# A two-block attention kernel on one core: the last 64 rows of keys and of queries as one chunk, another order of the jobs, and x's low halves earlier

## The chip, the cores and the metric

The kernel runs on one core of a Trainium2 chip. The metric is the time of one execution on the device, in microseconds, from the profiler; lower is better. The engines are TensorE (PE, its weight loads PEld), VectorE (DVE), ScalarE (ACT), GpSimd (POOL) and SyncE (SP), which here issues all transfers. Each engine runs its own list of instructions in order and waits for others by semaphores.

## The reference

64 independent sequences of 128 tokens, x (64, 128, 320) and a context of 128 tokens by 192. Two blocks, in float32:

```python
# block 0: attention over the context's first 124 tokens (8 heads of 40), a second one
# through its last 4 tokens, then a projection and the residual
query = hidden_states @ Wq
hs = _mha(query, enc @ Wk, enc @ Wv)
ca_q1 = jnp.einsum('btc,th->bch', ca, Wq_ca)[:, indices, :]
ca_hs1 = _mha(ca_q1, residual, residual)
ca_hs2 = _mha(ca_hs1 @ Wq, ca @ Wk_ca, ca @ Wv_ca)
out = (hs + ca_hs2) @ Wout + b_out + residual
# block 1: self attention, cross attention (20 heads of 16), gated feed-forward
h1 = _ln(x, n1_g, n1_b)
x = _attn(h1, h1, q1, k1, v1, o1_w, o1_b, heads) + x
h2 = _ln(x, n2_g, n2_b)
x = _attn(h2, context, q2, k2, v2, o2_w, o2_b, heads) + x
a, g = jnp.split(_ln(x, n3_g, n3_b) @ ff_w1 + ff_b1, 2, axis=-1)
x = a * gelu(g) @ ff_w2 + ff_b2 + x
```

## The kernel before

Two sequences make a step, so there are 32 steps, and the work of three stages is interleaved: while step i is in block 1's attention, the block 0 of the next step and the feed-forward of the step before run beside it. The program is a head (weights are scaled and split into a high and a low half of float16, so that a product in float16 passes comes near float32), step 0, step 1, a loop over 30 passes, step 32, and a tail with the last feed-forward. Steps 0, 1 and 32 are the loop's body with some jobs left out.

A step is a table of jobs, `BODY`, 128 of them. A job fills one of six PSUM banks in turn by matmuls and is evacuated by ScalarE, VectorE or both; a job waits until the job six places earlier in the table has been evacuated (`bank_free`, `last_on_bank`). So the table sets which job waits for which evacuation. The order of each engine's instructions is written out by hand, engine by engine, as calls such as `chunk16`, `scores` or `low_split`.

Names: Q0T k and K0T k are block 0's queries and keys, K1T k and Q1T k self attention's keys and queries, Q2T k and K2T k those of cross attention, each in chunks k = 0, 1, 2; those of block 1 have 128, 128 and 64 rows (`CH1`), a row being one column of a weight matrix. XT j_b are transposed norms (hTn), V0, V1, V2 values, S n and T n the scores for the maxima and for the exponents of unit n (units 0 to 3 the second attention of block 0, 4 to 13 self, 14 to 23 cross, 24 to 27 block 0's first), mx g the transposed maxima, ff t the feed-forward's first product, y b its second, outT and outM an attention's output and its projection, G the gains of the token queries. att is the product of exponents with values.

A chunk of K1T, Q1T or Q2T goes this way: 8 matmuls in `chunk16`; ScalarE writes its high half (`high_shifted`, L890), VectorE the whole value (`whole_shifted`, L1426), GpSimd the low half by a subtraction (`low_split`, L552), and SP spreads the heads over partitions by three transfers (`put_split`, `spread`, L406) into Ks or Qs, from where the scores read. `SPLITS_STEP` counts these chunks, 9 a step. Other GpSimd work named below: `low_probabilities` (L545) makes the low half of the exponents; `deviation` (L602, L603) the reciprocal deviation of a norm; `x_values` (L567 to L569), `token_queries` (L579 to L584, its last instruction writes ca_heads) and `low_x` (L592, the low half x16 of x) prepare the next step's block 0; the argument -1 means step 0, done in the head. `residual` (L1587) and `norm` (L1598) are VectorE's; `gelu` (L961) and `exps` (L977, L978) ScalarE's, which loads another function table between the two kinds.

Of the kernel before, what the change touches and what calls it, by code (L numbers as in the profile page):

```python
# [8 lines left out]
G = 2  # L9
# [83 lines left out]
SPLITS = {"K1T": 0, "Q1T": 3, "Q2T": 6}  # L93
SPLITS_STEP = 9
# [7 lines left out]
V1_FACTOR = 2.0 ** (V_EXP - math.floor(math.log2(1.01 * H * X_SCALE * 2.0 ** (W_EXP + 1))))  # L102

# [89 lines left out]
def build(nc, d, out):  # L193
# [4 lines left out]
    with ctx:  # L198
# [182 lines left out]
        def _(sp):  # L381
# [67 lines left out]
            def one_pass(i, stores, last=False):  # L449
# [4 lines left out]
                put_low(i, "Q0T", 2, Q0s, cQ, Q_PARTS)  # L454
# [2728 lines left out]
```

## Time and profile before

| | us |
|---|---|
| median of 3 runs | 3501.17 (3498.44 to 3502.05) |
| profiled execution | 3492.75 |
| its span, first to last instruction | 3490.9 |
| TensorE busy | 3261.7 (93%) |
| ScalarE busy | 2438.0 (70%) |
| VectorE busy | 2236.2 (64%) |
| GpSimd busy | 2022.1 (58%) |

All rows below come from the profiled execution, so sums are made against its 3492.75 us. Busy times overlap between engines. In a timeline, a row gives the start, the duration and the instruction, and in square brackets the engine's idle time before it with what ended it; rows of equal instructions are merged (x8). Matmuls are pipelined, so a row's duration contains some latency, and the distance between two starts is the time that TensorE spends.

### The profile page before, as it was taken

The numbers are of one execution on the slowest core, as the hardware profiler recorded it, in microseconds if no ns is written. First come the engines' busy times: TensorE is split into PE (matmuls) and PEld (weight loads), VectorE is DVE, ScalarE is ACT, GpSimd is POOL, SyncE is SP. The second block draws the span as 40 slices with busy tenths as digits, with TensorE's granted clock in tenths as the row PEclk, the third lists the DMA queues.
The fourth block names the chain that finished last, engine by engine and source line by source line (L and its number), as shares of the span: only waits on it lengthen the run. The fifth ranks groups of instructions, "written<-read, shape, count | busy, mean of one in ns | idle before, by whom it ended". The sixth has DMA issues, their size and how long they took to land.

```text
span 3490.9 us, 110595 instructions
## 1 busy us (share of the span) xinstructions
PE 3261.7 (93%) x37652; PEld 2674.3 (77%) x37652; DVE 2236.2 (64%) x5366; ACT 2438.0 (70%) x4279; POOL 2022.1 (58%) x2242
## 2 busy tenths in 40 slices
PE   7579999999999999999999999999999999999988
PEld 6367777787877778787777877777777777777766
DVE  6366666667666666766666676666667666666743
ACT  3257777777777777777777777777777777777753
POOL 1355656655665665566566555656655665665552
PEclk7589999999999999999999999999999999999998
DMA  6321111222111122222112222211222211122210
GB/s 196 63 51 44 52 41 45 50 50 57 48 52 42 44 50 51 56 48 54 40 45 50 53 54 48 54 39 45 50 50 57 48 51 41 45 51 50 57 35 19
DMA packets 314756, 181.21 MB, mean 52 GB/s; under 512 B 49740, under 2 KB 313900, under 8 KB 314028
## 3 DMA queue, kind: packets, MB, share of 16 engines
q1 hardware_dynamic: 302457, 172.71, 20.1%
q8 instruction: 323, 5.29, 0.6%
q10 hardware_dynamic: 11955, 3.04, 0.4%
q14 instruction: 21, 0.17, 0.0%
HBM read 69.36 MB, written 24.67 MB: 27 GB/s over the span
## 4 chain that ended last, share of the span: by engine, by line
PE 38%; POOL 26%; issue 26%; DVE 5%; ACT 2%; POOLq 1%; SPq 1%; DMA 1%; DVEq 1%; ACTq 0%
PE bank L2227 35%; POOL PT L545 15%; DVE mx L1525 2%; PE bank L2254 1%; POOL XB L522 1%; POOL XA L522 1%; POOL ca_heads L584 1%; POOL rstd L603 1%; POOL cQ L552 1%; POOL cK L552 1%; POOL c L597 1%; ACT P L977 1%; POOL rstd L602 1%; PE bank L2349 1%; ACT PT L978 1%
## 5 line engine op out<-in xcount | busy, mean ns | idle before, releaser
L545 POOL TENSOR_TENSOR PT<-P,PT 128x512 f16<-128x512 f32 (+1 forms) x896 | 1037.2, 1158 | 435.2 <-ACT PT L978 424.9
L1525 DVE TENSOR_REDUCE mx<-bank 128x4 f32<-128x512 f32 (+1 forms) x896 | 571.4, 680 | 92.0 <-PE bank L2227 88.6
L2227 PE MATMUL bank<-hT,w_ff_w 128*128 128x256 f16 x5120 | 611.1, 274 | 1.4 <-DVEq L1777 1.4
L2227 PEld LDWEIGHTS bank<-hT,w_ff_w 128*128 128x128 f16 x5120 | 498.5, 98 | 68.3 <-issue 6.2
L2227 PE MATMUL bank<-mxs,pick 84*128 84x128 f16 (+1 forms) x3584 | 506.9, 222 | 0.0
L2227 PE MATMUL bank<-w_ff,F 128*128 128x320 f32 x1280 | 393.3, 443 | 1.3 <-DVE F L1604 1.3
L2227 PEld LDWEIGHTS bank<-V,PT 128*128 128x128 f16 (+1 forms) x9216 | 315.3, 96 | 80.4 <-POOL PT L545 48.7
L2227 PEld LDWEIGHTS bank<-mxs,pick 84*128 84x128 f16 (+1 forms) x3584 | 368.3, 105 | 2.9
L2227 PE MATMUL bank<-Qs,Ks 96*128 96x128 f16 x2560 | 357.1, 222 | 9.1 <-DVE mxs L1534 8.8
L2227 PE MATMUL bank<-V,PT 128*128 128x17 f16 (+1 forms) x9216 | 343.3, 173 | 18.7 <-POOL PT L545 17.1
L961 ACT ACTIVATE gate<-bank,ff_b,scale 128x256 f32<-128x256 f32 x320 | 180.6, 564 | 215.0 <-PE bank L2227 175.1
L552 POOL TENSOR_TENSOR cQ<-whole,cQ 128x256 f16<-128x256 f32 (+1 forms) x192 | 128.2, 668 | 296.2 <-DVE whole L1426 287.9
L977 ACT ACTIVATE P<-bank,log_p,held 128x512 f32<-128x512 f32 x320 | 246.0, 769 | 71.8 <-PE bank L2227 40.9
L2227 PEld LDWEIGHTS bank<-w_ff,F 128*128 128x128 f32 x1280 | 227.2, 191 | 69.5 <-DVE F L1604 1.5
L2227 PEld LDWEIGHTS bank<-Qs,Ks 96*128 96x128 f16 x2560 | 247.0, 99 | 23.8 <-DVE mxs L1534 21.4
L977 ACT ACTIVATE P<-bank,log_p,exp_self 128x512 f32<-128x512 f32 x320 | 249.7, 780 | 15.0 <-PE bank L2227 5.5
L1426 DVE TENSOR_SCALAR whole<-bank,q_factor,qk_b 128x256 f32<-128x256 f32 (+1 forms) x288 | 155.8, 541 | 161.7 <-ACT cK L890 92.4
L1604 DVE SCALAR_TENSOR_TENSOR F<-bank,ff_b,gate 128x256 f32<-128x256 f32 x320 | 154.5, 483 | 156.4 <-ACT gate L961 145.8
L978 ACT ACTIVATE PT<-bank,log_p,exp_self 128x512 f16<-128x512 f32 x320 | 250.0, 781 | 0.0
L978 ACT ACTIVATE PT<-bank,log_p,held 128x512 f16<-128x512 f32 x320 | 245.7, 768 | 0.0
L938 ACT ACTIVATE hTn<-bank 128x384 f16<-128x384 f32 x320 | 153.8, 492 | 131.0 <-PE bank L2254 130.7
L2227 PE MATMUL bank<-Ks,Qs 96*128 96x128 f16 x2560 | 214.9, 221 | 17.1 <-DMA Qs<-cQ 12.9
(291 smaller groups left out, 7024.6 us busy)
## 6 DMA issues: line engine op xcount, KB each, us to landing
Qs<-cQ SPq DMA_DIRECT2D x402, 64.0 KB, 2.6
Ks<-scratch_k SPq DMA_DIRECT2D x99, 160.0 KB, 4.9
Ks<-cK SPq DMA_DIRECT2D x198, 64.0 KB, 2.6
Q0s<-cQ SPq DMA_DIRECT2D x198, 60.0 KB
K0s<-cK SPq DMA_DIRECT2D x198, 60.0 KB
xin<-in_x SPq DMA_DIRECT2D x33, 320.0 KB, 3.1
out<-X SPq DMA_DIRECT2D x64, 160.0 KB, 1.9
scratch_k<-cK SPq DMA_DIRECT2D x68, 128.0 KB, 1.9
```

The costliest lines, as they stand in the source:

```text
L522: nc.gpsimd.tensor_tensor(dst[:, b, :], src[:, b, :], bias[:, j, :], ALU.add).then_inc(ready, 1)
L545: nc.gpsimd.tensor_tensor(PT[0:keys, n % PT_SLOTS, 1, :], P[0:keys, n % P_SLOTS, :], PT[0:keys, n % PT_SLOTS, 0, :], ALU.subtract).then_in ...
L552: nc.gpsimd.tensor_tensor(dst[0:r, 1, k, :], whole[0:r, m % 3, :], dst[0:r, 0, k, :], ALU.subtract)\
L584: nc.gpsimd.tensor_tensor(ca_heads[:, :, :], ca16[:, :].unsqueeze(1).to_broadcast([rows, HEADS0, GS]), mask_ca[:, :].unsqueeze(2).to_broad ...
L938: nc.scalar.activation(dst[:, 0:3, b * S:(b + 1) * S], bank[:, 0:3 * S].rearrange("p (k s) -> p k s", k=3), ACT.Copy, scale=scaled).then_i ...
L961: nc.scalar.activation(gate[:, t % 2, :], bank[:, 0:GS], ACT.Gelu, scale=scale[:, 1:2], bias=ff_b[:, FFT + t:FFT + t + 1]).then_inc(a_done, 1)
L977: nc.scalar.activation(P[0:keys, n % P_SLOTS, :], bank[0:keys, :], ACT.Exp, bias=log_p[0:keys, :], scale=by)
L978: nc.scalar.activation(PT[0:keys, n % PT_SLOTS, 0, :], bank[0:keys, :], ACT.Exp, bias=log_p[0:keys, :], scale=by).then_inc(a_done, 1)
L1426: nc.vector.tensor_scalar(whole[0:r, m % 3, :], bank[0:r, 0:GS], q_factor[0:r, :], qk_b[0:r, c + k:c + k + 1], ALU.mult, ALU.add).then_inc ...
L1525: nc.vector.tensor_reduce(mx[:, g % 2, 4 * u:4 * u + 4], bank[:, :].rearrange("p (h s) -> p h s", h=4)[:, :, 0:keys], axis=AX.X, op=ALU.ma ...
L1604: nc.vector.scalar_tensor_tensor(out=F[:, t, :], in0=bank[:, GS:2 * GS], scalar=ff_b[:, t:t + 1], in1=gate[:, t % 2, :], op0=ALU.add, op1= ...
L2227: return nc.tensor.matmul(o, lhsT, rhs, start=start, stop=stop)
```

## The change

Self attention's last chunks of keys and queries, 64 rows each, become one chunk of 128 rows: the last 64 columns of q1 are appended to k1's, so that the chunk K1T2 holds 64 key rows and below them 64 query rows, and job Q1T2 with its evacuations is gone (127 jobs, 8 splits). The three transfers for Q1T2 stay and read rows 64 to 127 of cK. The jobs and every engine's list get another order. In the head, GpSimd makes x's values and low halves before it waits for the last weights.

```diff
-SPLITS = {"K1T": 0, "Q1T": 3, "Q2T": 6}
-SPLITS_STEP = 9
+SPLITS = {"K1T": 0, "Q1T": 3, "Q2T": 5}
+SPLITS_STEP = 8
+
+COLUMNS = {"ff_w1": 2 * FF, "k1": H + CH1[2], "q1": H - CH1[2]}
...
+def rows_of(name, k):
+
+    return S if (name, k) == ("K1T", 2) else CH1[k]
...
-    Q0T0 Q0T1 S0 S1 ff0 Q0T2 XT0_0 XT0_1 ff1 V0_0 mx0 K1T0 K1T1 T0 S2 K1T2 Q1T0 S3 ff2 Q1T1 ff3 ff4
-    Q1T2 K0T0 mx1 T1 vca S4 S5 V1_0 T2 S6 S7 T3 S8 S9 mx2 S10 K0T1 T4 T5 S11 V1_1 T6 S12 T7 S13 caT0
...
+    ff0 Q0T0 XT0_0 S0 XT0_1 Q0T1 V1_0 S1 Q0T2 K1T0 S2 K1T1 K1T2 mx0 Q1T0 Q1T1 S3 T0 T1 ff1 ff2 mx1
+    ff3 ff4 S4 S5 T2 vca S6 S7 T3 S8 S9 mx2 S10 S11 T4 S12 T5 S13 V1_1 T6 mx3 caT0 T7 T8 caT1 K0T0
+    T9 T10 T11 T12 s4 T13 mT ff5 ff6 mB outT1_0 ff7 outT1_1 K0T1 outM1_0 outM1_1 K0T2 V0_0 ff8 XT1_0
+    XT1_1 ff9 Q2T0 Q2T1 Q2T2 V0_1 K2T0 S14 S15 y1 S16 S17 S18 S19 mx4 S20 S21 S22 S23 T14 S24 K2T1
+    T15 S25 mx5 T16 T17 T18 S26 T19 T20 mx6 T21 T22 y0 T23 S27 p4T V2_0 outT2_0 T24 mx7 T25 outM2_0
+    outT2_1 T26 T27 hs0 outM2_1 outT0_0 hs1 V2_1 outM0_0 outT0_1 XT2_0 XT2_1 G K2T2 outM0_1
...
             def put_split(i, name, k, dst, src, parts):
                 if (name, k) == ("K1T", 0):
                     sp.wait_ge(j_full, done(i - 1, LOOP_JOBS.number("T23"), "J"))
-                sp.wait_ge(split_done, (i + 1) * SPLITS_STEP + SPLITS[name] + k + 1)
-                spread(name, k, dst, src, D1, CH1, parts)
+                if (name, k) == ("Q1T", 2):
+                    sp.wait_ge(split_done, (i + 1) * SPLITS_STEP + SPLITS["K1T"] + 3)
+                    spread(name, k, dst, cK, D1, CH1, parts, CH1[2])
+                else:
+                    sp.wait_ge(split_done, (i + 1) * SPLITS_STEP + SPLITS[name] + k + 1)
+                    spread(name, k, dst, src, D1, CH1, parts)
...
                 put_low(i, "Q0T", 0, Q0s, cQ, Q_PARTS)
                 put_low(i, "Q0T", 1, Q0s, cQ, Q_PARTS)
-                put_low(i, "Q0T", 2, Q0s, cQ, Q_PARTS)
                 put_split(i, "K1T", 0, Ks, cK, K_PARTS)
...
                 if not last:
                     load_next(i)
+                put_low(i, "Q0T", 2, Q0s, cQ, Q_PARTS)
+                stack_cross_keys(i)
...
+            pool.wait_ge(step_loaded, LOADS_STEP)
+            pool.wait_ge(next_ready, 1)
+            pool.drain()
+            for b in range(G):
+                x_values(-1, b, X4)
+            low_x(-1)
             pool.wait_ge(low_ready, 1)
...
-            for b in range(G):
-                x_values(-1, b, X4)
             token_queries(-1)
-            low_x(-1)
...
+    p["k1"] = np.concatenate([p["k1"], p["q1"][:, AT1[2]:H]], 1)
+    p["q1"] = p["q1"][:, 0:AT1[2]]
```

The first place where the order differs is TensorE's list at the start of a loop pass. A row is a line of the program, the operation, the bank and what goes in; x16 with w16_Wq is Q0T, hT3 with w16_ff_w1 is ff, ident with OA is XT0, G16 with ca_heads is S, hTn with w16_v1 is V1 and with w16_k1 is K1T. Before:

```order
L2227 MATMUL bank0<-x16,w16_Wq 120x256 x8
...
L2227 MATMUL bank1<-x16,w16_Wq 120x256 x8
...
L2227 MATMUL bank2<-G16,ca_heads 128x128 x4
...
L2227 MATMUL bank4<-hT3,w16_ff_w1 128x256 x16
L2227 MATMUL bank5<-x16,w16_Wq 80x256 x8
...
L2254 MATMUL bank0<-ident,OA 128x128 x3
...
L2227 MATMUL bank5<-hTn,w16_k1 128x256 x8
```

After:

```order
L2238 MATMUL bank0<-hT3,w16_ff_w1 128x256 x16
...
L2238 MATMUL bank1<-x16,w16_Wq 120x256 x8
...
L2265 MATMUL bank2<-ident,OA 128x128 x3
...
L2238 MATMUL bank3<-G16,ca_heads 128x128 x4
...
L2265 MATMUL bank4<-ident,OA 128x128 x3
...
L2238 MATMUL bank5<-x16,w16_Wq 120x256 x8
...
L2238 MATMUL bank0<-w16_v1,hTn 128x320 x8
```

ff0 is the first job now and follows outM0_1, whose bank it takes; the transposes XT0 and V1_0 stand further ahead, K1T0 further back. 

The second place is GpSimd's list from the step's first bias additions to the second low probabilities (L522 and L534 are bias additions, L552 and L564 the subtractions of `low_split`, L545 and L557 the low probabilities; step 1 is shown, the loop has the same order). Before:

```order
L552 TENSOR_TENSOR cK<-whole,cK 128x256 x2
L522 TENSOR_TENSOR XB<-XA,bias 128x320
L552 TENSOR_TENSOR cK<-whole,cK 64x256
L522 TENSOR_TENSOR XA<-xin,bias 128x320
L552 TENSOR_TENSOR cQ<-whole,cQ 128x256 x2
L545 TENSOR_TENSOR PT<-P,PT 128x512
L552 TENSOR_TENSOR cQ<-whole,cQ 64x256
```

After:

```order
L564 TENSOR_TENSOR cK<-whole,cK 128x256
L534 TENSOR_TENSOR XB<-XA,bias 128x320
L564 TENSOR_TENSOR cK<-whole,cK 128x256 x2
L564 TENSOR_TENSOR cQ<-whole,cQ 128x256
L534 TENSOR_TENSOR XA<-xin,bias 128x320
L557 TENSOR_TENSOR PT<-P,PT 128x512
L564 TENSOR_TENSOR cQ<-whole,cQ 128x256
```

The 64-row subtractions of this attention are gone, and the second one for the queries (Q1T1) stands behind the first low probabilities.

The third place is GpSimd's list in the head, from the last clearing that waits for nothing. Before:

```order
L627 MEMSET X 128x640
L630 MEMSET XA 128x640
...
L630 MEMSET OB 128x640
...
L567 TENSOR_TENSOR X<-xin,next_factor 128x320
...
L579 TENSOR_TENSOR ca<-ca,next_factor 96x256
...
L584 TENSOR_TENSOR ca_heads<-ca,mask_ca 96x2048
L592 TENSOR_TENSOR x<-xT,x 128x768
```

After:

```order
L639 MEMSET X 128x640
...
L579 TENSOR_TENSOR X<-xin,next_factor 128x320
...
L604 TENSOR_TENSOR x<-xT,x 128x768
L648 MEMSET XA 128x640
...
L648 MEMSET OB 128x640
L591 TENSOR_TENSOR ca<-ca,next_factor 96x256
...
L596 TENSOR_TENSOR ca_heads<-ca,mask_ca 96x2048
```

The clearing of XA, which waits for the last weights, and the token queries now stand behind x's values and low halves.

At the end of a step, GpSimd's `token_queries` moves from ahead of the two `deviation` calls of the next norms to behind `x_values`, and `low_x` moves from ahead of `x_values` to between those two calls. On TensorE, K2T2 moves to the step's end between G and outM0_1, K2T1 behind S24, ff5 and ff6 ahead of the last products of self attention, and y1 ahead of S16. On ScalarE, the splitting of the context follows Q0T1 and both exponents of T0 and of T1 stand ahead of the gelu of ff1.

## Rows read from the trace of the kernel before

**Rows 1.** The page, part 1: busy us (share of the span) x instructions

```profile
PE 3261.7 (93%) x37652; PEld 2674.3 (77%) x37652; DVE 2236.2 (64%) x5366; ACT 2438.0 (70%) x4279; POOL 2022.1 (58%) x2242
```

**Rows 2.** Stretches: head, step 0, loop; length, busy by engine, clock, DMA

```profile
0.00:110.00 110.00, 73.91 (x297) 65.07 (x298) 66.63 (x182) 35.48 (x64) 30.16 (x28) 0.67 0.53 164
110.00:184.00 74.00, 49.02 (x408) 34.49 (x408) 24.96 (x61) 23.36 (x46) 26.86 (x27) 0.61 0.32 62
...
288.00:3343.00 3055.00, 2931.13 (x34860) 2413.68 (x34860) 2029.68 (x4860) 2258.64 (x3961) 1862.39 (x2070) 1.00 0.20 49
```

**Rows 3.** TensorE's waits in the loop: total us, times, longest us

```profile
PE bank L2349 <- DVE mx L1525: 57.1, 90, 0.8
PE bank L2227 <- DVE G L1439: 18.6, 30, 0.6
PE bank L2227 <- POOL PT L545: 10.5, 29, 0.4
PE bank L2227 <- DVE hTn L1554: 9.8, 31, 0.3
...
PE bank L2227 <- DMA Qs<-cQ: 4.8, 6, 1.1
```

**Rows 4.** Timeline of TensorE in one pass: chunks of self attention

```profile
1220.27 1.05 PE L2227 MATMUL bank<-hTn,w_q 128*128 128x256 f16 x8
...
1227.59 1.06 PE L2227 MATMUL bank<-hTn,w_q 128*64 128x256 f16 x8
1228.58 0.76 PE L2227 MATMUL bank<-c,w_Wk 128*120 128x256 f16 x5
```

**Rows 5.** Timeline of VectorE at the start of that pass

```profile
1207.67 0.48 DVE L1439 SCALAR_TENSOR_TENSOR G<-bank,fixed,G 32x256 f16<-32x256 f32 x1
1208.18 0.55 DVE L1587 SCALAR_TENSOR_TENSOR XA<-bank,factor,XA 128x320 f32<-128x320 f32 x1
...
1209.45 0.41 DVE L1598 TENSOR_SCALAR OA<-XA,mv,rstd 128x320 f32<-128x320 f32 x1
1210.58 1.09 DVE L1598 TENSOR_SCALAR OA<-XA,mv,rstd 128x320 f32<-128x320 f32 x1 [0.71 <-POOL rstd L603]
```

**Rows 6.** Timeline of GpSimd in that pass: subtraction and low probabilities

```profile
1226.46 0.67 POOL L552 TENSOR_TENSOR cQ<-whole,cQ 128x256 f16<-128x256 f32 x1 [1.21 <-DVE whole L1426]
1227.09 1.16 POOL L545 TENSOR_TENSOR PT<-P,PT 128x512 f16<-128x512 f32 x1
```

**Rows 7.** Timeline of TensorE: the first job of that pass

```profile
1208.20 1.96 PE L2227 MATMUL bank<-x,w_Wq 128*120 128x256 f16 x16 [0.62 <-DVE G L1439]
```

**Rows 8.** Timeline of ScalarE in that pass: gelu and exponents

```profile
1212.46 1.28 ACT L961 ACT_TABLE_LOAD   x1 [0.59 <-PE bank L2227]
1213.76 0.57 ACT L961 ACTIVATE gate<-bank,ff_b,scale 128x256 f32<-128x256 f32 x1
...
1220.60 0.78 ACT L977 ACTIVATE P<-bank,log_p,factor 128x512 f32<-128x512 f32 x1
```

**Rows 9.** Timeline of SP's transfer issues in that pass

```profile
1225.77 6.74 SPq L406 DMA_DIRECT2D Qs<-cQ  x9
```

**Rows 10.** The page, part 6: issues, KB each, us to landing

```profile
Qs<-cQ SPq DMA_DIRECT2D x402, 64.0 KB, 2.6
```

**Rows 11.** Timeline of GpSimd at the start of that pass

```profile
1204.16 3.60 POOL L584 TENSOR_TENSOR ca_heads<-ca,mask_ca 96x2048 f16<-96x2048 f16 x1
1207.72 0.19 POOL L602 TENSOR_TENSOR rstd<-mv,eps 128x1 f32<-128x1 f32 x1
```

**Rows 12.** Timeline of GpSimd in the head

```profile
95.12 0.63 POOL L630 MEMSET XA<- 128x640 f32 x1 [16.55 <-DVE ff_b L1755]
...
104.33 3.60 POOL L584 TENSOR_TENSOR ca_heads<-ca,mask_ca 96x2048 f16<-96x2048 f16 x1
107.89 1.63 POOL L592 TENSOR_TENSOR x<-xT,x 128x768 f16<-128x768 f32 x1
```

**Rows 13.** Timeline of TensorE at the head's end

```profile
109.77 3.26 PE L2227 MATMUL bank<-x,w_Wq 128*120 128x256 f16 x16 [15.83 <-POOL x L592]
```

More of the change, by code:

```diff
@@ L399, in stack, with spread @@
                                  src[part, :, :].rearrange("(h e) n -> e h n", e=e)).then_inc(landed, 16)
-            def spread(name, k, dst, src, e, rows, parts):
+            def spread(name, k, dst, src, e, rows, parts, row=0):
                 heads = rows[k] // e
@@ L405, in spread @@
                 for y, part in enumerate(parts):
-                    sp.dma_start(dst[y * e:(y + 1) * e, at:at + heads, :], src[0:rows[k], part, k, :])\
+                    sp.dma_start(dst[y * e:(y + 1) * e, at:at + heads, :],
+                                 src[row:row + rows[k], part, k, :])\
                         .then_inc(stacked[name][k], 16)
@@ L692, in _ @@
             left_out(i, pool_done_by=1, rstd_ready_by=1)
-            token_queries(i)
             deviation(i, 0, 0)
+            low_x(i)
             deviation(i, 0, 1)
@@ L728, in _ @@
             low_split(i, "Q2T", 1, cQ)
+            second_bias(i, 0)
+            x_values(i, 0, OA)
             low_split(i, "Q2T", 2, cQ)
-            second_bias(i, 0)
-            low_x(i)
-            x_values(i, 0, OA)
             x_values(i, 1, OA)
+            token_queries(i)
             low_probabilities(i, 14)
@@ L750, in _ @@
             deviation(i, 2, 1)
-            token_queries(i)
             deviation(i, 0, 0)
+            low_x(i)
             deviation(i, 0, 1)
@@ L786, in _ @@
                 low_split(i, "Q2T", 1, cQ)
+                second_bias(i, 0)
+                x_values(i, 0, OA)
                 low_split(i, "Q2T", 2, cQ)
-                second_bias(i, 0)
-                low_x(i)
-                x_values(i, 0, OA)
                 x_values(i, 1, OA)
+                token_queries(i)
                 low_probabilities(i, 14)
@@ L808, in _ @@
                 deviation(i, 2, 1)
-                token_queries(i)
                 deviation(i, 0, 0)
+                low_x(i)
                 deviation(i, 0, 1)
@@ L2052, in _ @@
-                residual(i, 1, 0)
-                low_out(i, 1, 1)
-                norm(i, 1, 0)
-                ff(i, L, 6)
-                residual(i, 1, 1)
+                ff(i, L, 5)
+                normalise(i, 3)
+                ff(i, L, 6)
+                step_sizes(i, L)
+                low_out(i, 1, 0)
+                ff(i, L, 7)
+                low_out(i, 1, 1)
+                low_chunk(i, "K0T", 1, cK, CH0[1], FK0)
+                residual(i, 1, 0)
+                residual(i, 1, 1)
@@ L2616, in _ @@
+            exponents(i, 24)
             turn_maxima(i, 7)
-            chunk(i, "K2T", 2, "k2", c16, PASSES_C, AT1, CH1)
-            exponents(i, 24)
-            left_out(i, pv_done_by=1)
             exponents(i, 25)
-            left_out(i, pv_done_by=1, j_full_by=2)
-            values(i, "V2", 0, "v2")
+            left_out(i, pv_done_by=2, j_full_by=2)
             exponents(i, 26)
@@ L2743, in _ @@
             scores(i, 22)
+            scores(i, 23)
             exponents(i, 14)
-            scores(i, 23)
             scores(i, 24)
+            chunk(i, "K2T", 1, "k2", c16, PASSES_C, AT1, CH1)
             exponents(i, 15)
```

1129 lines of the change are left out of this document (557 added, 572 removed).

## Prediction

> **What bounds the kernel now.** I read the busy shares first [rows 1], then the stretches [rows 2], then the waits of TensorE in the loop [rows 3]. TensorE is busy 93% of the span, ScalarE 70%, VectorE 64%, GpSimd 58%. The stretches say where the rest is: the head up to 110 us, with the granted clock at 0.67 of full speed (a mean of its two levels, 1.2 and 2.4 GHz); step 0, 74 us at 0.61; and 30 loop passes in 3055 us, 101.8 us each, at the full 2.4 GHz, where TensorE is busy 2931 us (96%). So in the loop TensorE's own work sets the time. Its idle 124 us is 4.1 us a pass and is spread: 57.1 us for the maxima on VectorE (1.9 a pass, three transposes of maxima), 18.6 for VectorE's token heads G (0.62), 10.5 for the low probabilities on GpSimd (0.35), 9.8 for the normalised transposes hTn (0.33), 4.8 for the spreads of Qs (0.16) [rows 3]. The head is not TensorE's: it stands 15.8 us for x16, which GpSimd writes last.
>
> **The sum is made against the profiled execution**, 3492.75 us; the median of the timed runs is 8.4 us above it (3501.17), and I put those 8.4 us back at the end. A measurement of this kernel can tell about 0.2% (7 us) from no change; "same" below means that.
>
> **1. One chunk instead of two.** A chunk of keys or queries is 8 matmuls over 256 columns, and it is busy as long with 64 output rows (1.06 us) as with 128 (1.05); the removed chunk of 64 query rows starts at 1227.59 and its successor at 1228.58, so it holds TensorE for 0.99 us [rows 4]. It is removed in steps 1 to 32: 32 x 0.99 = 31.7 us of TensorE. With it go one evacuation on ScalarE, one on VectorE (each about as long as G's 0.48 [rows 5]) and one subtraction on GpSimd (0.67 [rows 6]) a step, all on engines with room; I cost them at nothing, since TensorE's next work covers them. The three spreads of the removed chunk remain, read from other rows of cK, so SP's queue gets no shorter.
>
> **2. The start of a pass.** Two waits go. G's evacuation no longer stands ahead of the first matmul (0.62 [rows 3, 7]), because ff0 and not Q0T0 is first; and K1T0 comes three jobs later, so hTn is there (0.33). One comes: ff0 uses the bank of outM0_1, the job just ahead of it, and has to wait until VectorE's residual(0,1) has read it. That is at least the residual's own 0.55 us; if G (0.48) and the evacuation of K2T2's tokens (priced as G, 0.48) stand ahead of it, 1.5 [rows 5]. Before, the residual ended 0.5 us after the first matmul of the pass had begun [rows 5, 7], so the truth is nearer the lower end: 0.9. Another: V1_0 needs XT0_0's transposes evacuated, and on ScalarE these stand behind ff0's gelu with its table load, 1.28 + 0.57 = 1.85 us [rows 8], to which come two evacuations on ScalarE and VectorE each, while TensorE has two chunks (1.98 us) and three short jobs to do. Between 0 and 1.0: 0.4. Sum of this place: 0.9 + 0.4 - 0.62 - 0.33 = +0.35 us a pass.
>
> **3. Self attention's stacks.** On GpSimd the subtraction for Q1T1 now stands behind the first low probabilities; before it stood ahead. So the last spread of Qs hangs on T0: table load 1.28, two exponents of 0.78 [rows 8], the low probabilities 1.16, the subtraction 0.67 [rows 6], six spreads at 6.74/9 = 0.75 (4.5) [rows 9], and 2.6 us to land [rows 10]: some 11.8 us. TensorE's work between T0 and S8 is four fillings of the feed-forward (16 matmuls each, as long as two chunks: 7.9 us), one job of exponents, five of scores, one of token values and a few products: an estimate of 11 us. So there is no slack and little excess: 0 to 0.8, against 0.16 that is there now. In exchange Q0T2's three issues leave SP's queue ahead of Ks (they now stand behind load_next), which brings the first stacks about 2.3 us forward. Taken: no net change.
>
> **4. The end of self attention and cross attention.** ff5 and ff6 now stand ahead of the last products of self attention, which covers the 0.35 us for low probabilities. Of the transposes of maxima, mx5 gets K2T1 and T14 as cover, and mx4 loses cover, since y1 moves ahead of S16: together I add 0.2 to the 1.9 us, with 0 and 0.8 (the longest such wait [rows 3]) as ends. Sum: -0.15 a pass.
>
> **5. GpSimd's step end.** token_queries (one of its instructions alone is 3.60 us) stood ahead of the two deviations of the next norms, and deviation(0,0) began as it ended [rows 11]. Now it stands between x_values and the low probabilities of cross attention, beside the maxima there. It can delay the first of these; I price that at 0 to 0.5 us (the wait on low probabilities that a pass now has is 0.35 [rows 3]) and take 0.2. At the step's end norm(0,0), and so XT0_0, can begin earlier; that gives back at least part of the 0.4 us that V1_0's wait costs in 2, and I take 0.2 to 0.6, 0.4. low_x (1.63 us [rows 12]) now stands between the two deviations; I cost it at nothing and say in the rivals what it costs if that is wrong. Sum: -0.2 a pass.
>
> The waits of a pass: +0.35 + 0 - 0.15 - 0.2, no net change. So a pass is 0.99 us shorter: 100.8 us. The ends named above, set against the gains, give -0.9 to +1.5 us a pass.
>
> **6. The head.** GpSimd waits 16.55 us, until 95.1, for the last weights' low halves, then clears four tiles, makes x's values, the token queries (ca_heads 3.60 at 104.33) and x16 (1.63 at 107.89), and TensorE begins at 109.77 [rows 12, 13]. From 97.5, behind the clearing, to ca_heads' first steps the values take some 4.7 us and x16 1.63: 6.3 us that go into that wait, if their own inputs are there by 95.1 - 6.3 = 88.8, which I take to be so. Behind the wait remain the clearing and the token queries, so ca_heads ends at about 109.5 - 6.3 = 103.2, and Q0T0, which wants no ca_heads, can begin at about 98. The scores S0 need both and come 9 to 10 us earlier. SP's spreads of Q0s wait for their chunk, and the loads for step 1 stand behind them in its queue: both come earlier by as much, unless SP is still at earlier work. What is late next: these spreads and stacks, since step 0 is a chain of transfers and small work at half clock. Bounds: 3 us (only part of the way is on the path) to 12 us (all, and the token queries out of step 0's end too). Taken: 7 us, near the 6.3 of moved work. Step 1 gains 1 us from the shorter SP queue ahead of its first stack. Together -8.
>
> **Sum.** 3492.75 - 31.7 - 8 = 3453; with 8.4 for the median, **3462 us**.
>
> **The rivals.**
> - *Absorbed.* The 0.99 us are given back because what follows waits on other engines (maxima, exponents). Then only the head is left: 3501 - 8 = 3493. For it: 1.9 us a pass are waits on maxima [rows 3] that VectorE sets. Against it: the removed chunk stands at none of these waits, and 96% busy leaves 4.1 us a pass in all. The Trainium skill, *Perfetto Trace Analysis*, section Identifying the Most-Contended Engine, says that matmul busy time is no good measure for TensorE, and that weight loads' busy share and the achieved rate are. By that share (PEld, 77% [rows 1]) TensorE would have room, and this rival's 3493 would be the time. The row on start times [rows 4] is no busy time but a distance of starts, and speaks against it.
> - *The waits shrink too*, at -0.9 us a pass: 3462 - 29 = 3433.
> - *The new waits at the start of a pass are dear*: low_x on GpSimd beside norm(0,0) on VectorE. The norm took 0.41 us where GpSimd did little and 1.09 beside GpSimd's bias additions [rows 5]. If norm(0,0) stretches so, XT0_0 and with it V1_0 are later by 0.68: 32 x 0.68 = 22, 3484. If it waits for the whole of low_x, 1.63 us [rows 12], the time is 3462 + 32 x 1.63 = 3514. The rows show a stretch of 0.68 and no wait of that length. The Trainium skill, *SBUF — State Buffer*, section SBUF: two separate sides, has GpSimd and some VectorE operations take turns on a shared port pair, the loser blocked for a whole instruction, which would be the second of these two; the rows agree that the norm suffers and not that it is blocked.
> - *Slower.* Q1T1's subtraction behind the low probabilities makes S6 and S8 wait. The place: GpSimd's queue between T0 and S8, with ScalarE's table load and SP's six spreads behind it (11.8 us, step 3). Each us of wait is 30 us of time; from 1.5 us a pass more than I took, the kernel is slower than before. If ScalarE takes the exponents of T0 only after the gelu of ff1 is asked for, or SP's spreads stand behind late ones, 2.5 us: 3462 + 75 = 3537. Against it: ScalarE's order has both exponents of T0 ahead of ff1's gelu.
>
> **How the numbers follow.** Chances: the forecast 0.54, with 3445 to 3480 from the ends of the head (12 and 3 us for 8) and half of those of the waits; the waits shrink 0.14; the dear start 0.13, of which 0.03 for a norm that waits for all of low_x; absorbed 0.10; slower 0.09. The likeliest gives 3462. The range leaves out the slower case, 3514 and the lower part of the second: 3427 to 3494. Faster by over 0.2% is below 3494: 0.54 + 0.14 + 0.10 + 0.04 of the absorbed case, 0.82. Slower by as much is above 3508: 0.09 + 0.03, 0.12. The same: 0.06, the rest of the absorbed case.
>
> **What would show it.** Per pass, the distance of two ca_heads or two first matmuls: 100.8 us instead of 101.8. In the waits of TensorE: G and hTn gone, a new wait of ff0 for residual XA of about 0.9 us, V1_0 for hTn of 0 to 1, Qs under 0.8 a pass. First Q0T0 at about 98 us, first scores of step 0 at about 103. Wrong would be: a pass of 101.5 or more with a wait for Qs or XA over 1.5 us, or a step 0 that ends where it did.

## The result

The changed kernel takes 3643.52 us (median; 3632.5 to 3651.1) against 3501.61 us for the kernel before on the same chip: a ratio of 1.0406, interval 1.0386 to 1.0426. It is 142 us slower; forecast was 3462 us, faster. Its profiled execution took 3642.2 us, with a span of 3640.4.

The page's first part (busy us, share of the span, instructions), against [rows 1]:

```profile
PE 3303.0 (91%) x37388; PEld 2714.3 (75%) x37388; DVE 2206.8 (61%) x5335; ACT 2403.5 (66%) x4247; POOL 1998.1 (55%) x2210
```

TensorE has 264 matmuls fewer (32 chunks of 8, and 8 small ones outside the loop), and is busy 41 us longer. Stretches of the kernel after (length; busy us and instructions of TensorE, weight loads, VectorE, ScalarE, GpSimd; granted clock; DMA share; GB/s): the head, step 0, two passes in a row, and a window of the loop. They answer to [rows 2]:

```profile
0.00:98.00 98.00, 71.61 (x290) 63.31 (x290) 67.00 (x169) 33.95 (x61) 23.19 (x18) 0.69 0.55 175
98.00:180.10 82.10, 50.81 (x390) 34.80 (x390) 27.05 (x70) 23.04 (x47) 33.73 (x35) 0.54 0.28 65
...
1045.50:1157.20 111.70, 103.25 (x1155) 85.64 (x1154) 66.71 (x162) 74.43 (x132) 61.26 (x68) 0.92 0.19 45
1157.20:1260.10 102.90, 96.26 (x1156) 79.31 (x1155) 66.70 (x162) 74.15 (x132) 61.29 (x68) 1.00 0.20 49
300.00:3300.00 3000.00, 2777.05 (x32272) 2291.71 (x32270) 1860.61 (x4497) 2072.88 (x3659) 1715.97 (x1904) 0.96 0.19 47
```

The same window of the kernel before:

```profile
300.00:3300.00 3000.00, 2878.34 (x34277) 2371.54 (x34276) 1993.16 (x4774) 2220.49 (x3891) 1824.55 (x2028) 1.00 0.21 49
```

The passes are not alike. The second of the two passes above runs at the full 2.4 GHz, with TensorE busy 96.26 us; the first, of the same instructions, is busy 103.25 us at a mean clock of 0.92 and takes 9 us more. GpSimd writes the token heads (ca_heads) once a pass, and their distance averages 107.16 us over 29 passes (before: 101.83): 22 of 30 are over 105 us, none under 102.2. From the end of step 1 to that of step 31 (outM0_1) the 30 passes take 155.7 us more than before, and the rest of the program takes 6.2 us less: the loss is all in the loop. TensorE's waits in that window (total us, times, longest us), against [rows 3]:

```profile
PE bank L2238 <- DVE mxs L1545: 56.8, 28, 3.4
PE bank L2238 <- DMA Qs<-cQ: 45.7, 46, 1.6
PE bank L2362 <- DVE mx L1536: 41.2, 80, 0.9
PE bank L2238 <- DVE XA L1598: 27.5, 28, 1.0
PE bank L2238 <- DVE hTn L1565: 26.9, 27, 1.0
PE bank L2265 <- DVE OA L1651: 11.1, 28, 0.4
PE bank L2238 <- ACT gate L976: 6.2, 8, 0.8
```

3000 / 107.16 is 28.0 passes, so a pass waits 2.0 us for mxs (the evacuated maxima), 1.6 for Qs, 1.5 for mx, 1.0 for XA, 1.0 for hTn, 0.4 for OA, 0.2 for the gelu: 7.7 us. In the kernel before, the same view sums to 4.0 a pass. That is +3.7. The rest of the +5.3 is TensorE itself: 2777.05 / 28.0 = 99.2 us busy a pass, against 2878.34 / 29.5 = 97.7, although a chunk of 0.99 us is gone.

**The longest wait, row by row.** mxs is VectorE's evacuation of the transpose mx3, which T9 wants. In VectorE's list `extremes_x(i+1)` stands ahead of it, in both kernels: it reduces the next step's x, and waits for all ten loads of that step, of which x (xin) is issued last. SP starts them when VectorE has read the token values (vca). First the kernel before: SP's issues of the loads, the first and the last; VectorE; TensorE at T9 (start us, duration, engine, line, operation, tiles, [idle before <- releaser]):

```profile
1232.99 0.74 SPq L384 DMA_DIRECT2D xT<-in_xT  x1
...
1238.57 0.40 SPq L391 DMA_DIRECT2D xin<-in_x  x1
```

```profile
1242.62 0.81 DVE L1451 TENSOR_REDUCE ext_wide<-xin 128x1 f32<-128x640 f32 x1
...
1243.98 0.28 DVE L1534 SCALAR_TENSOR_TENSOR mxs<-bank,mxs 20x128 f16<-20x128 f32 x1
```

```profile
1242.76 0.28 PE L2349 MATMUL bank<-ident,mx 128*20 128x128 f32 x1
...
1244.32 0.23 PE L2227 MATMUL bank<-Qs,Ks 96*128 96x128 f16 x1 [0.20 <-DVE mxs L1534]
```

mx3 comes 9.8 us after the first load; x is there, and VectorE doesn't wait. The same three views of the kernel after, in the shorter of the two passes above:

```profile
1186.62 0.56 SPq L391 DMA_DIRECT2D xT<-in_xT  x1
...
1192.76 0.40 SPq L398 DMA_DIRECT2D xin<-in_x  x1
```

```profile
1195.80 0.82 DVE L1462 TENSOR_REDUCE ext_wide<-xin 128x1 f32<-128x640 f32 x1 [1.37 <-DMA xin<-in_x]
1196.63 0.28 DVE L1545 SCALAR_TENSOR_TENSOR mxs<-bank,mxs 20x128 f16<-20x128 f32 x1
```

```profile
1192.59 0.27 PE L2362 MATMUL bank<-ident,mx 128*20 128x128 f32 x1
...
1197.06 0.22 PE L2238 MATMUL bank<-Qs,Ks 96*128 96x128 f16 x1 [1.08 <-DVE mxs L1545]
```

mx3 now comes 6.0 us after the first load, since the new order takes V1_0 and K0T1 out of the stretch between vca and mx3 and puts vca behind S4, S5 and T2. VectorE waits for x, and T9 for VectorE. In a longer pass of the same kernel mx3 is as far from the first load (3212.21 to 3218.18), but x is issued 6.6 us after it, not 6.1, and VectorE starts on it 4.2 us after that, not 3.0. Then something else follows. VectorE and TensorE there, and seven stretches of 3 us around it (columns as above):

```profile
3223.00 0.82 DVE L1462 TENSOR_REDUCE ext_wide<-xin 128x1 f32<-128x640 f32 x1 [2.98 <-DMA xin<-in_x]
```

```profile
3224.27 0.22 PE L2238 MATMUL bank<-Qs,Ks 96*128 96x128 f16 x1 [2.69 <-DVE mxs L1545]
```

```profile
3218.00:3221.00 3.00, 2.95 (x55) 2.67 (x53) 1.25 (x4) 3.00 (x7) 2.31 (x3) 1.00 0.71 206
3221.00:3224.00 3.00, 0.57 (x5) 0.33 (x3) 0.98 (x2) 2.24 (x4) 2.55 (x3) 1.00 0.27 77
3224.00:3227.00 3.00, 2.73 (x41) 2.68 (x42) 2.25 (x7) 0.66 (x1) 0.12 (x1) 0.60 0.00 0
3227.00:3230.00 3.00, 3.00 (x31) 3.00 (x28) 0.00 (x0) 2.13 (x4) 1.95 (x2) 0.50 0.00 0
3230.00:3233.00 3.00, 3.00 (x41) 2.75 (x41) 1.24 (x6) 1.80 (x3) 0.64 (x2) 0.50 0.04 9
3233.00:3236.00 3.00, 3.00 (x31) 2.34 (x29) 0.41 (x1) 1.15 (x3) 2.03 (x2) 0.69 0.75 139
3236.00:3239.00 3.00, 3.00 (x56) 2.67 (x54) 0.00 (x0) 2.97 (x4) 1.16 (x1) 1.00 0.75 83
```

After a wait of 2.69 us TensorE works on, fully busy, at 1.2 GHz for some 10 us, and that costs about 1.2 + 1.5 + 1.5 + 0.9 = 5 us (each stretch's length times what its clock lacks to 1.00). After the wait of 1.08 us the clock stayed up. Over the 30 passes: T9 waits 2.06 to 3.42 us in 17, and each of these waits is followed by some 10 us at 1.2 GHz; it waits 0.24 to 1.33 us in the other 13, and three of those (1.10, 1.14 and 1.33 us) are followed by some 7 us of it. The Trainium skill, *TensorE: Matmul & The Clock Gate*, section HAM oscillation — how this bites in real kernels, tells of a kernel whose loop waits for a transfer in each tile and begins the next one at half clock; these rows agree.

So the first theory is **T**: the x load on VectorE ahead of mx3 costs 2 us a pass in waiting and about 3 more through the clock. Rivals: **Q**, the waits for Qs that the prediction's slower case named; **S**, the waits at the start of a pass (XA, hTn).

### The profile page after: what moved, and what is told of

It reads as the page before. It is cut to its first block, busy times and chain, and to the rows that moved or that the text cites. A ratio compares the mean times of both kernels' runs of the same rounds, so it can differ in the third digit from the quotient of the medians.

```text
span 3640.4 us, 109680 instructions
## 1 busy us (share of the span) xinstructions
PE 3303.0 (91%) x37388; PEld 2714.3 (75%) x37388; DVE 2206.8 (61%) x5335; ACT 2403.5 (66%) x4247; POOL 1998.1 (55%) x2210
## 4 chain that ended last, share of the span: by engine, by line
issue 32%; PE 28%; POOL 21%; DVE 7%; SPq 4%; DMA 4%; ACT 4%; POOLq 1%; ACTq 1%; DVEq 0%
PE bank L2238 26%; POOL PT L557 10%; DVE mx L1536 2%; SPq L413 2%; DMA Qs<-cQ 2%; POOL rstd L615 2%; POOL cQ L564 2%; DMA xin<-in_x 1%; ACT PT L993 1%; POOL XB L534 1%; POOL x L604 1%; ACT P L992 1%; POOL cK L564 1%; POOL rstd L614 1%; POOL X L534 1%
## 5 line engine op out<-in xcount | busy, mean ns | idle before, releaser
L557 POOL TENSOR_TENSOR PT<-P,PT 128x512 f16<-128x512 f32 (+1 forms) x896 | 1035.6, 1156 | 655.8 <-ACT PT L993 640.2
L2238 PE MATMUL bank<-hT,w_ff_w 128*128 128x256 f16 x5120 | 628.7, 280 | 33.9 <-DVE XA L1598 30.5
L1536 DVE TENSOR_REDUCE mx<-bank 128x4 f32<-128x512 f32 (+1 forms) x896 | 580.4, 681 | 63.3 <-PE bank L2238 58.8
L2238 PE MATMUL bank<-mxs,pick 84*128 84x128 f16 (+1 forms) x3584 | 534.7, 231 | 0.0
L2238 PE MATMUL bank<-Qs,Ks 96*128 96x128 f16 x2560 | 385.1, 233 | 59.0 <-DVE mxs L1545 59.0
L2238 PEld LDWEIGHTS bank<-mxs,pick 84*128 84x128 f16 (+1 forms) x3584 | 382.7, 109 | 2.0
L2238 PEld LDWEIGHTS bank<-Qs,Ks 96*128 96x128 f16 x2560 | 261.3, 104 | 76.5 <-DVE mxs L1545 65.5
L614 POOL TENSOR_TENSOR rstd<-mv,eps 128x1 f32<-128x1 f32 x192 | 43.3, 226 | 417.3 <-DVE mv L1603 417.2
L2238 PE MATMUL bank<-Ks,Qs 96*128 96x128 f16 x2560 | 201.5, 223 | 69.1 <-DMA Qs<-cQ 58.5
L2238 PEld LDWEIGHTS bank<-Ks,Qs 96*128 96x128 f16 x2560 | 157.7, 99 | 115.4 <-DVE mx L1536 43.0
L1545 DVE SCALAR_TENSOR_TENSOR mxs<-bank,mxs 8x128 f16<-8x128 f32 (+1 forms) x256 | 72.2, 282 | 231.8 <-ACT mxs L966 216.0
```

Source lines behind the costliest of these rows:

```text
L557: nc.gpsimd.tensor_tensor(PT[0:keys, n % PT_SLOTS, 1, :], P[0:keys, n % P_SLOTS, :], PT[0:keys, n % PT_SLOTS, 0, :], ALU.subtract).then_in ...
L614: link(i, nc.gpsimd.tensor_tensor(rstd[:, j, b:b + 1], mv[:, j, b, 1:2], eps[:, :], ALU.add))
L1536: nc.vector.tensor_reduce(mx[:, g % 2, 4 * u:4 * u + 4], bank[:, :].rearrange("p (h s) -> p h s", h=4)[:, :, 0:keys], axis=AX.X, op=ALU.ma ...
L2238: return nc.tensor.matmul(o, lhsT, rhs, start=start, stop=stop)
```

## The experiments

Each is timed against the kernel before on its own chip; an interval follows each ratio. "The window" is 300 to 3300 us throughout.

**The extremes moved.** In the kernel after, on VectorE:

```diff
-                extremes_x(i + 1)
                 low_maxima(i, 3)
                 ...
                 low_chunk(i, "K0T", 0, ...)
+                extremes_x(i + 1)
```

> The changed kernel, with one VectorE instruction moved: the size of the next step's x (extremes_x, which waits for the load of xin) stands behind the evacuation of the transposed maxima mx3 instead of ahead of it. Theory A (the wait of the exponents T9 is VectorE held by that load, and TensorE's clock falls because of this wait): T9's wait of 1.3 to 2.9 us goes, the clock stays at full speed in the loop, a pass takes about 101 us instead of 107.1, in all about 3460 us. Rival B (the chain of exponents on ScalarE behind the late stacks makes T9 wait): no change, 3640. Rival C (T9's wait is the load, but the clock falls for another reason of the new order): passes of about 105.5, in all about 3590.

3500.83 us, ratio 1.0012 (0.9998 to 1.0026). The mxs wait is gone, the clock in the window is 0.99, a pass averages 102.78 us (the profiled execution is the slowest of the ten, 3518.05 us). One line moved on an engine that is busy 61% takes off some 140 us. T holds; Q and S are not what made the kernel slow, since their waits are still there (Qs 35.6, XA 28.3 and hTn 28.9 us in the window). The 3460 us expected with T did not come: 41 us are missing, and the kernel is only as fast as the one before.

**The load moved.** The same with VectorE's order left as it was: x gets a semaphore of its own and is loaded first.

```diff
+                sp.wait_ge(xa_ready, i * G + G)
+                sp.wait_ge(vx_ready, i * G + G)
+                load_x(i + 1)
                 ... (wait for vca, then the other nine loads)
-                dve.wait_ge(step_loaded, i * LOADS_STEP + LOADS_STEP)
+                dve.wait_ge(x_loaded, i * LOADS_X + LOADS_X)
```

> The changed kernel with its order of engines untouched; only the load of x (xin) is issued ahead of the nine other loads of a step and doesn't wait for vca, with a semaphore of its own. Theory A: x lands some 5 us earlier, before VectorE asks for it, so T9's wait and the falls of the clock go as in the run with the moved instruction: about 101 us a pass, 3460 in all. Rival B: 3640. Rival C: 3590.

3492.94 us, ratio 0.9992 (0.9981 to 1.0003), no pass over 105.0 us. It is the load, then, and not the reduction's 0.8 us. Here too 33 us are missing to 3460; the repairs below ask where they are. The Trainium skill, *DMA: Bandwidth & Descriptors*, section Why a DMA increments its semaphore by 16 and not by 1, says that of several transfers in flight on one semaphore a count doesn't tell which has landed; that is why x needs its own here. What no run shows is the stale data that the page warns of.

**The clock's part.** Two runs, one from each side. In the kernel after, K0T0's chunk, which stands just ahead of T9, is computed five times into its bank, so that TensorE works while it would have waited; four of the five are extra work, some 0.6 us each:

```diff
-                chunk(i, "K0T", 0, "Wk", c16, PASSES_C, AT0, CH0)
+                chunk_again(i, 5)
```

> The changed kernel; in the loop the chunk K0T0 ahead of the exponents T9 is multiplied five times instead of once into the same bank, so that TensorE is busy during T9's wait for VectorE. The wait's cause is untouched. Theory A1 (the clock falls because TensorE stands idle in this wait): the clock stays at full speed, and although 2.4 us of matmuls a pass are added, a pass takes about 104.5 us instead of 107.1, in all about 3565. Rival C (the clock falls for another reason): 3642 or more.

And in the kernel before, four reductions with no reader (2.8 us) ahead of `low_maxima(i, 3)` on VectorE:

```diff
+                for k in range(4):
+                    nc.vector.tensor_reduce(ballast[:, k:k + 1], cT[:, :, :], axis=AX.XY, op=ALU.max, ...)
```

> The kernel before; in the loop VectorE makes four reductions of 0.69 us for nothing ahead of the evacuation of the maxima mx3 (2.8 us). Theory A1: T8's wait grows from 0.35 to about 3 us, TensorE's clock falls after it as in the changed kernel, and a pass takes 2.8 + 4 to 5 us more: about 3700. Rival C: only the delay itself, 30 x 2.8: 3580 to 3585.

The window of the kernel with the wait filled, and then the wait and the window of the kernel with the delay:

```profile
300.00:3300.00 3000.00, 2820.76 (x33464) 2341.85 (x33462) 1897.29 (x4578) 2119.17 (x3730) 1740.82 (x1931) 0.99 0.21 48
```

```profile
PE bank L2230 <- DVE mxs L1535: 75.1, 28, 3.8
...
300.00:3300.00 3000.00, 2820.91 (x32395) 2331.26 (x32393) 1949.72 (x4611) 2105.96 (x3679) 1721.27 (x1916) 0.96 0.20 47
```

More work made the kernel after faster: 3584.42 us, ratio 1.0218 (1.0203 to 1.0234), some 60 us less, at a clock of 0.99; mxs is down from 56.8 to 13.8 us in the window, and the other waits stayed. That is near the 3565 expected. And a delay alone made the kernel before slow: 3667.15 us, ratio 1.0471 (1.0455 to 1.0487), where the delay by itself would have made 3585. Its pass is 107.64 us, 5.8 more, of which the longer wait is 75.1 / 27.9 - 8.2 / 29.5 = 2.4 us (8.2 us is mxs in the kernel before) and TensorE's longer busy time 101.2 - 97.7 = 3.5. A wait of 2.7 us in the middle of dense work thus costs more than twice its length.

**The merged chunk alone**, in the kernel before (no new order, head as before): Q1T2 leaves the list of jobs, K1T2 has 128 rows.

```diff
-    Q1T2 K0T0 mx1 T1 vca S4 S5 V1_0 T2 ...
+    K0T0 mx1 T1 vca S4 S5 V1_0 T2 ...
```

> The kernel before with the merged chunk alone: K1T2 of 128 rows, no Q1T2, every order otherwise as before, the head too. The prediction's first term: 0.99 us of TensorE less in each of 32 steps, about 3470 us (3460 to 3485 with moved bank waits). Rival (absorbed by waits on other engines): 3500.

3532.1 us, ratio 1.0103 (1.0084 to 1.0121): taking 0.99 us of work out of a pass makes it 1.4 us longer. The new wait, in the window:

```profile
PE bank L2235 <- DVE XA L1599: 34.9, 29, 1.2
```

TensorE's six banks go round, job n using bank n mod 6. A step had 128 jobs and has 127. 127 mod 6 is 1, so the first job of a pass gets the bank of the job just ahead of it, outM0_1, and waits for its residual. Next, the same with another order of the banks: a queue of six, from which four jobs of a step take the second bank and not the first, so that a pass begins with five jobs or more between two uses.

```diff
+EARLY = (11, 64, 69, 116)
+        banks.append(queue.pop(1 if n in EARLY else 0))
-                return j_bank[n % J_BANKS]
+                return j_bank[BANK[n]]
```

> The kernel before with the merged chunk alone (as in the run before, 3532 us), and with another order of the six PSUM banks: with 127 jobs the plain rotation gives the first job of a pass the bank of the last one, a distance of 1; here one bank is taken one job earlier at four places, so that no job waits for one nearer than 5 places back. Theory D (the merge alone is slower because of this seam): Q0T0's wait for the residual XA, 36 us in the loop, goes, and what else follows from it; 3475 to 3500. Rival E (the merge is slower because Q1T2's work no longer covers the way of the stacks and the maxima): the waits for Qs and mxs stay at 32 and 17 us, and the time stays above 3515.

3489.69 us, ratio 0.9973 (0.9958 to 0.9989), XA gone. The seam was worth some 42 to 46 us in that order (by medians and by ratios). Of the 32 us that the merge takes out, 9 to 14 arrive: Qs now waits 49.7 us in the window (before: 4.8). That the last three spreads now come from the merged chunk is a likely reason; it wasn't tried.

**The head alone**, in the kernel before:

```diff
+            for b in range(G):
+                x_values(-1, b, X4)
+            low_x(-1)
             pool.wait_ge(low_ready, 1)
             ... (the four clearings)
-            (x_values and low_x behind them)
             token_queries(-1)
```

> The kernel before with the head's change alone: GpSimd makes x's values and low halves before it waits for the last weights. The prediction's sixth term: step 0 begins about 10 us earlier and 7 us (3 to 12) remain: about 3494. Rival: step 0 gives all of it back, because its transfers or a lower clock set its end: 3501.

3498.14 us, ratio 1.0002 (0.9991 to 1.0012): nothing. TensorE in that run, first job and M's product, then M's product in the kernel before:

```profile
103.56 3.64 PE L2228 MATMUL bank<-x,w_Wq 128*120 128x256 f16 x16 [8.31 <-DVE G L1440]
...
143.99 2.74 PE L2228 MATMUL bank<-M,whole 120*128 120x32 f32 x12 [1.08 <-DVE whole L1545]
```

```profile
145.14 2.74 PE L2227 MATMUL bank<-M,whole 120*128 120x32 f32 x12 [1.08 <-DVE whole L1544]
```

The first job is 6.2 us earlier (109.77 in [rows 13]), M's product 1.15.

**Repairs.** The kernel after with x loaded first, banks as above (four other jobs), Q0T1 ahead of XT0_1, and V1_0 behind ff4:

```diff
-    ff0 Q0T0 XT0_0 S0 XT0_1 Q0T1 V1_0 S1 Q0T2 K1T0 ...
+    ff0 Q0T0 XT0_0 S0 Q0T1 XT0_1 S1 Q0T2 K1T0 ...
-    ff3 ff4 S4 S5 T2 vca ...
+    ff3 ff4 V1_0 S4 S5 T2 vca ...
```

> The changed kernel with three repairs: x's load early as in the second run, the banks' order with no distance under 5, and two jobs moved (Q0T1 ahead of XT0_1; V1_0 behind ff4, just ahead of S4). If the waits at the start of a pass and at S4 are what gives the merged chunk's gain back: ff0's wait of 1.1 us, V1_0's of 1.2 and S4's of 0.9 go, and of these about 2.5 us a pass are kept: some 3420 (3400 to 3460). Rival (the chain from outM0_1 over the norms and the stacks to S4 sets the time, not TensorE's order): the waits come back at XT0_1, K1T0 or S4, 3480 to 3495.

3465.88 us, ratio 0.9901 (0.9887 to 0.9915): faster than both kernels, but 46 us above the 3420 expected. hTn, 28.9 us in the window with the load alone moved, is 40.0, now in front of K1T0; and a wait that the trace gives no releaser for stands inside ff0. To part the three, only the first two:

> The changed kernel with two of the three repairs of the run before: x loaded first, and the order of the banks with which ff0 no longer waits for residual XA. Theory A (waits that stand in a row add up): of the run with the early load alone (3492.9) ff0's wait, 31.0 us in all, comes off: about 3462, and moving V1_0 and Q0T1, the third repair, was worth nothing. Theory B (one wait takes over another's time): ff0 begins earlier and V1_0's wait for hTn, 30.5 us, grows by as much, to 60: about 3490, and the third repair is worth some 25 us.

3483.35 us, ratio 0.9951 (0.9935 to 0.9968): between the two expectations, and neither mechanism. One pass's start, and the window's row:

```profile
1198.09 0.93 PE L2257 MATMUL bank<-hT,w_ff_w 128*128 128x256 f16 x7
1199.64 1.14 PE L2257 MATMUL bank<-hT,w_ff_w 128*128 128x256 f16 x9 [0.63 <-issue]
```

```profile
PE bank L2257 <- issue: 28.7, 29, 1.4
```

ff0 no longer waits for XA (28.3 us in the window with the load alone moved) and now stands in its middle, for as long. The wait for XA had covered that stall; so the seam, worth 42 us in the old order, is worth 10 to 14 here (3492.94 to 3483.35).

The view says only that no semaphore explains the stall. The transfers of the same trace say more. On the page, q8 is the queue that loads instructions, in pieces of 16 KB: 323 packets in the kernel before, 352 in the kernel after and in this one, 29 more. In the pass shown, one of them runs from 1197.45 to 1198.38 (`--dma --window 1197.4:1198.4` has that packet alone), and ff0 goes on at 1199.64, 1.26 us after its end. So it is in all 29 passes of this run and all 29 of the three repairs: such a transfer begins 1.1 to 1.9 us ahead of the stall, takes 0.88 to 1.48 us, and ff0 goes on 1.2 to 1.6 us after its end, while the stall itself varies from 0.4 to 1.4 us. In the kernel after, ff0 begins some 1 us later behind the same transfer, and no stall is seen. That TensorE stands for its instructions there is thus likely, but not tested: no run moved the place where a pass begins.

**Two of GpSimd's moves undone**, in the kernel with the three repairs. Q1T1's subtraction ahead of the first low probabilities:

```diff
                 low_split(i, "Q1T", 0, cQ)
+                low_split(i, "Q1T", 1, cQ)
                 zero_bias(i, 0)
                 low_probabilities(i, 0)
-                low_split(i, "Q1T", 1, cQ)
```

> The kernel with all three repairs (3465.9), but with GpSimd's subtraction for Q1T1 ahead of the first low probabilities, as in the kernel before. The prediction's slower rival said that this order makes S6 and S8 wait. Theory A (S6 to S9 never wait, their trace shows no stall there, and the only wait for Qs in a pass is S16's of 0.64 us): no change, 3462 to 3470, and Qs stays at about 15 us in the loop. Rival: the last spreads do bind through the queue behind them, and the time falls by over 10 us.

3462.08 us, ratio 0.9889 (0.9873 to 0.9906), Qs 18.5 us in the window against 14.7: no difference from the repairs. And Q2T2's subtraction ahead of x's values:

```diff
                 low_split(i, "Q2T", 1, cQ)
+                low_split(i, "Q2T", 2, cQ)
                 second_bias(i, 0)
                 x_values(i, 0, OA)
-                low_split(i, "Q2T", 2, cQ)
```

> The kernel with all three repairs (3465.9), but with GpSimd's subtraction for Q2T2 directly behind that for Q2T1, as in the kernel before, and no longer behind a bias addition and x's values. Theory A: S16's wait for Qs (0.64 us a pass, 14.7 us in the loop's rows) goes, and mx4, which waits 1.0 us for VectorE right behind it, takes it over: 3460 to 3468. Theory B: the waits add up, S16's 0.64 us times 32 comes off: 3445.

3463.8 us, ratio 0.9896 (0.9879 to 0.9912). The window's waits with the three repairs, and below with this undone:

```profile
PE bank L2379 <- DVE mx L1555: 49.1, 82, 0.9
...
PE bank L2255 <- DMA Qs<-cQ: 14.7, 30, 0.5
```

```profile
PE bank L2379 <- DVE mx L1555: 68.9, 81, 1.5
```

Qs is gone and mx has grown by 19.8 us: the transpose of maxima mx4, which follows, took the wait over. The scores that waited for Q2T2 are those of unit 18 (S18), the first to read its heads, and not S16, as the last two expectations have it.

## Why the prediction was wrong

- **What failed.** The sum has no term for mx3. Step 3 took the stretch of self attention in which vca and mx3 stand, and asked only what the new order does to GpSimd, SP's spreads and Qs; step 4 priced the maxima mx4 and mx5. So the wait of T9 for mx3 was put at nothing, with no reason given, and it cost 2.0 us a pass in waiting and about 3 through the clock. The step to be taken was to list what VectorE has ahead of mx3: `extremes_x`, with its wait for the loads. It had no price, since in the trace of before it didn't wait. But its slack could have been worked out: x is issued at 1238.57 and lands 3.1 us later by the page's sixth part, VectorE starts on it at 1242.62, about 1 us; and the order of the jobs showed the stretch from vca to mx3 getting shorter, by 3.8 us as it turned out. Moving either the load or the reduction takes off some 140 to 150 us.
- **The clock.** The prediction counted waits one for one and took the loop's 2.4 GHz [rows 2] as given. Even with the 2 us of mxs in a term, the 3 of the clock would have been missing.
- **The gain failed too.** With x loaded first the long wait is gone, and the kernel is as fast as the one before (0.9992), where the sum had 40 us of gain. In that run's window the waits still sum to 5.3 us a pass, against 4.0 before, which takes back the chunk's 0.99, and the clock of 0.99 costs about 0.4 more.
- **1, one chunk.** Right as TensorE's own work: 0.99 us of starts [rows 4], and the pass at full clock is busy 96.26 us, against 97.7. In the old order the seam of 127 jobs gave it back and more. The prediction did see that ff0 gets outM0_1's bank, and sized that in step 2 at 0.9; 1.0 was measured.
- **2, the start of a pass.** The signs were right. G and its 0.62 are gone [rows 3, 7]. V1_0 waits 1.0 us, not 0.4, the upper end that was named. Each move was costed by itself: with XA's wait taken away, ff0 stalled for as long.
- **3, the stacks.** "No net change" was wrong by 1.5 us a pass, but not at S6 to S9, which never waited, and not through the order on GpSimd, whose undoing changed nothing. Of the 45.7 us in the window, 19.8 are S4, the first scores (20 passes, 0.5 to 1.2 us each), although SP's queue ahead of their spreads got shorter; 25.9 are S18 (26 passes, 0.5 to 1.6 us), which waits for Q2T2's subtraction, behind x's values. So the slower rival named a wait that came, 58.5 us for Qs in the whole execution, with another place and mechanism; it is not what made the 142.
- **4 and 5.** mx fell from 1.9 to 1.5 us a pass instead of rising by 0.2; PT fell from 10.5 us [rows 3] to nothing in the window, as said. The absorbed rival came true in part, though at Qs and not at the maxima that it named: with the seam mended 9 to 14 of 32 us arrived. The dear start did not come: in a pass of the kernel after, low_x ran on GpSimd from 1158.96 to 1160.60 and the norm kept its 0.42 us behind it.

```profile
1162.41 0.42 DVE L1609 TENSOR_SCALAR OA<-XA,mv,rstd 128x320 f32<-128x320 f32 x1
```

- So low_x and the norm did not meet in the loop, and the 0.41 of [rows 5] is there again. But GpSimd and VectorE did meet in the head, through the change itself, and the sum had no term for that.
- **6, the head.** Q0T0 came at 102.49 for 98, S0 at 107.81 for 103, both 4.5 to 5 us late, since VectorE's work on the last weights ends later than before and GpSimd's clearing with it. TensorE and GpSimd in the kernel after:

```profile
102.49 1.94 PE L2238 MATMUL bank<-x,w_Wq 128*120 128x256 f16 x8
...
107.81 0.61 PE L2238 MATMUL bank<-G,ca_heads 96*128 96x128 f16 x4 [3.27 <-POOL ca_heads L596]
```

```profile
99.59 0.63 POOL L648 MEMSET XA<- 128x640 f32 x1 [5.33 <-DVE ff_b L1765]
```

- The clearing began at 95.12 before [rows 12] and begins at 99.59. The reason is on VectorE, which scales weights while GpSimd now makes x's values and low halves. VectorE in the kernel before, then VectorE and the last of GpSimd's moved instructions in the kernel after:

```profile
86.36 2.86 DVE L1733 SCALAR_TENSOR_TENSOR w_o_w<-raw_o_w,gains,w_o_w 128x320 f16<-128x320 f32 x6
89.14 1.47 DVE L1733 SCALAR_TENSOR_TENSOR w_Wq<-raw_Wq,gains,w_Wq 128x320 f16<-128x320 f32 x3
```

```profile
86.56 5.22 DVE L1743 SCALAR_TENSOR_TENSOR w_o_w<-raw_o_w,gains,w_o_w 128x320 f16<-128x320 f32 x6
91.71 3.37 DVE L1743 SCALAR_TENSOR_TENSOR w_Wq<-raw_Wq,gains,w_Wq 128x320 f16<-128x320 f32 x3
92.39 1.88 POOL L604 TENSOR_TENSOR x<-xT,x 128x768 f16<-128x768 f32 x1
```

- These nine instructions take 4.3 us longer, and GpSimd's clearing, which waits for the end of VectorE's list of weights, is late by as much; with the head alone they take the same 5.22 and 3.37 us. VectorE's instruction that began at 92.69, 0.3 us into GpSimd's of 1.88 us, took 1.93 us, against 0.55 before. The Trainium skill, *SBUF — State Buffer*, section SBUF: two separate sides, has GpSimd and some VectorE operations take turns on a shared port pair, the loser blocked for a whole instruction; these rows agree. The prediction read its own rows as speaking against such a block; the head's rows speak for it.
- With the head alone, what was earlier is given back by 144 us, in the wait for VectorE ahead of M's product. In the kernel after, M's product is still 5.3 us earlier (139.86 for 145.14), and step 0's last product, outM0_1, 0.6 us (182.35 for 182.98). Of the -8, 0.6 came.
- **The range.** 3427 to 3494 held what the forecast's order could do once mended (3462 to 3493), not what it did. The range was built from the ends of the terms that had been listed; the miss was a term not listed.

What stays open: whether the stall inside ff0 is the wait for instructions that it looks like, and why x lands 1 us or more later in most passes than in others, which decides how far the clock falls. The trace gives a hint for x. In 14 of the 17 passes with a long wait of T9, a 16 KB transfer of the instruction queue begins 0.9 to 1.6 us after x's issue, as x is being moved; in the 13 others it begins 2.2 us or more after it. In the two passes shown above it is 1.45 us (longer) and 2.50 us (shorter). No run tried it.

## What to carry to other kernels

When an order changes, list for every engine what stands ahead of each job that the bounding engine waits for, with the waits that are zero now: write down their slack (here about 1 us) and how much the new order takes away (3.8). When a job leaves a rotation of buffers, work out the seam between two passes again, and expect a wait that is removed to uncover the next one. One long wait is dearer than several short ones of the same sum (here waits of up to 1.5 us that sum to 5.3 us a pass left the clock at 0.99, one of 2.7 us a pass brought it to 0.96): if it can't be removed, break it up or fill it. And work that is moved into an engine's idle time can slow the engine that it was waiting for.

## What the runs showed of the hardware

- TensorE's clock fell after one wait of 2.69 us in otherwise dense work and took some 10 us to come back; so it did after all 17 waits of 2.06 us or more at that place, and for some 7 us after 3 of 13 waits of up to 1.33 us. In the delayed kernel before, where that wait averaged 2.7 us, all 30 passes were over 105 us.
- Extra matmuls in place of most of such a wait made a kernel 1.6% faster (3643.5 to 3584.4 us).
- A job's stall of about 1 us after 7 or 9 of its 16 matmuls, which no semaphore explains, came in all 29 passes of the window once the job's own wait was gone. It ended 1.2 to 1.6 us after a 16 KB transfer of the instruction queue had, in every one of 58 passes of two runs.
- Nine instructions of VectorE, 4.33 us alone, took 8.59 us beside GpSimd's in the head; one of 0.55 us took 1.93 beside one of 1.88.
